# Routing to the experts in every second slot: eleven steps of a top-4 choice spread over nineteen slots of a pipelined kernel

## What is computed

```python
h = _layernorm(x) * (1 + ca) + sa
x = x + ga * attention(h)          # top 2 of 8 experts; chunks of linear attention, 8 heads
h = _layernorm(x) * (1 + cb) + sb
h = h @ lin0_w + lin0_b
h = _silu(h @ swi1_w1 + swi1_b1) * (h @ swi1_w2 + swi1_b2)
# the mixture of the feed-forward half
scores = softmax(h @ gate_w.T)
topv, topi = top_k(scores, 4)
topv = topv / sum(topv)
combine = zeros((t, 8)).at[arange(t)[:, None], topi].set(topv)
g = _silu(einsum('td,edh->eth', h, exp_w1))
u = einsum('td,edh->eth', h, exp_w3)
routed = einsum('te,etd->td', combine, einsum('eth,ehd->etd', g * u, exp_w2))
shared = _silu(h @ sh_w1) * (h @ sh_w3) @ sh_w2
h = (routed + shared) @ lin1_w + lin1_b
h = _silu(h @ swi2_w1 + swi2_b1) * (h @ swi2_w2 + swi2_b2)
x = x + gb * h
```

## Time and profile before

| what | us |
|---|---|
| median of three runs | 1185.22 |
| lowest and highest | 1184.74, 1187.0 |
| the profiled execution | 1182.44 |
| its span, first to last instruction | 1180.7 |
| TensorE busy in the span | 1038.6 |
| VectorE busy | 889.3 |
| ScalarE busy | 651.6 |
| GpSimd busy | 508.5 |

### The profile page before, as it was taken

The page is one execution under the profiler, slowest core; times in us unless marked ns, Lnnn a source line. Parts: engine busy times, 40 slices in busy tenths (PEclk is TensorE's granted clock), DMA queues, the critical chain, the costliest instruction groups (busy, mean ns, idle before and its releaser), DMA issues.

```text
span 1180.7 us, 26036 instructions
## 1 busy us (share of the span) xinstructions
PE 1038.6 (88%) x8950; PEld 759.1 (64%) x8950; DVE 889.3 (75%) x2067; ACT 651.6 (55%) x1596; POOL 508.5 (43%) x464
## 2 busy tenths in 40 slices
PE   4776778889998888999899898978998899899997
PEld 3554556656666665667666666756776677677774
DVE  3775576889996577778778887788778877886764
ACT  2432444445554555766567564756776665555564
POOL 2217144431224443221222126767886554455552
PEclk9787899999998999999999999999999999999999
DMA  8982133333332332222222116330532233225230
GB/s 232 399 349 94 67 108 104 108 101 91 99 106 91 95 100 86 68 61 71 66 71 66 56 42 177 90 94 25 158 103 59 65 100 99 61 67 151 80 90 18
DMA packets 81134, 123.08 MB, mean 104 GB/s; under 512 B 8944, under 2 KB 63728, under 8 KB 76912
## 3 DMA queue, kind: packets, MB, share of 16 engines
q1 hardware_dynamic: 70768, 96.24, 26.4%
q0 software_dynamic: 10240, 25.18, 6.8%
HBM read 70.27 MB, written 51.12 MB: 103 GB/s over the span
## 4 chain that ended last, share of the span: by engine, by line
PE 57%; DVE 23%; ACT 7%; issue 7%; another core or an unknown queue 5%; SPq 0%; DMA 0%; POOL 0%; DVEq 0%; ACTq 0%; POOLq 0%
PE wide L1410 7%; PE bank L1670 6%; PE wide L1660 6%; PE bank L1660 6%; PE bank L1385 6%; PE bank L1470 5%; PE bank L1454 3%; DVE epp L1746 3%; DVE att L1512 3%; DVE kvw L1753 2%; PE bank L963 2%; PE bank L1462 2%; PE bank L1399 2%; PE bank L1372 1%
## 5 line engine op out<-in xcount | busy, mean ns | idle before, releaser
L1625 POOL TENSOR_TENSOR kvw<-kvw,hq 128x512 f32<-128x512 f32 x128 | 173.0, 1352 | 153.0 <-ACT kvw L1713 152.7
L1512 DVE SCALAR_TENSOR_TENSOR att<-reach,endrel,wide 128x1024 f32<-128x1024 f32 x152 | 194.5, 1280 | 52.9 <-PE wide L1410 33.6
L885 POOL DMA_INDIRECT gst<-attended_rows,idxs x128 | 134.0, 1047 | 215.7 <-DVE att L1512 108.2
L255 POOL DMA_INDIRECT routed_rows<-hq,idxs x128 | 127.0, 992 | 220.0 <-DVE att L1512 110.6
L1746 DVE TENSOR_TENSOR epp<-kvw,epp 128x512 fp32r<-128x512 f32 x160 | 134.9, 843 | 87.0 <-ACT epp L1721 84.6
L1670 PE MATMUL bank<-epp,w2p 128*128 128x512 f32 x480 | 163.5, 449 | 11.1 <-DVE epp L1746 11.1
L1721 ACT ACTIVATE epp<-kvw 128x512 fp32r<-128x512 f32 x160 | 100.7, 629 | 84.5 <-DVE kvw L1753 80.1
L1660 PE MATMUL bank<-hp,w1p 128*128 128x512 f32 x480 | 138.1, 396 | 0.0
L1660 PE MATMUL wide<-hp,w3p 128*128 128x512 f32 x480 | 136.6, 393 | 0.0
L1385 PE MATMUL bank<-kvw,turned 128*128 x304 | 129.1, 507 | 3.8 <-ACT turned L1275 1.6
L1410 PE MATMUL wide<-turned,kx 32*128 32x128 f32 x2432 | 112.5, 298 | 21.2 <-DVE att L1512 19.5
(11 more groups left out here) (267 smaller groups left out, 1878.0 us busy)
## 6 DMA issues: line engine op xcount, KB each, us to landing
hq<-weight_rows SPq DMA_DIRECT2D x16, 2048.0 KB
rows<-routed_rows SPq DMA_DIRECT2D x76, 256.0 KB
routed_rows<-zero SPq DMA_DIRECT2D x2, 7168.0 KB, 34.1
attended_rows<-ob SPq DMA_DIRECT2D x76, 128.0 KB
routed_rows<-zero SPq DMA_DIRECT2D x1, 5120.0 KB, 17.4
out<-fin SPq DMA_DIRECT2D x16, 256.0 KB, 2.3
routed_rows<-hq,idxs POOLq DMA_INDIRECT x128
gst<-attended_rows,idxs POOLq DMA_INDIRECT x128
```

What stands on the lines that cost most here:

```text
L255: pool.indirect_dma_start(hs[s], bass.IndirectOffsetOnAxis(idxs[:, t, k:k + 1], 0), hq[:, t, :], None, bounds_check=BLOCKS[s] * P - 1, oob ...
L885: pool.indirect_dma_start(gst[:, u, k, :], None, orow[s], bass.IndirectOffsetOnAxis(idxs[:, t, k % TOPA:k % TOPA + 1], 0), bounds_check=BL ...
L1512: dve.scalar_tensor_tensor(out=att[:, n % 2, :, :], in0=reach[:, :, :].rearrange("p a c -> p (a c)").unsqueeze(1) .to_broadcast([P, 4, 2 * ...
L1625: pool.tensor_tensor(g, g, rows_of(1 - b % 2, n, n + 1), ALU.mult).then_inc(s_eu, 1)
```

## The change

Part p of a group's routing stood p slots behind the group's step 0. It now stands 1 + floor(9 (p - 1) / 5) slots behind: steps 1, 2, 4, 6, 8, 10, 11, 13, 15, 17 and 19 for parts 1 to 11. The exponential (step 2) and the turn of the weights (step 21) stay.

```diff
             for part in range(1, 12):
-                r = group(part, slot)
+                r = group(1 + (part - 1) * 9 // 5, slot)
                 if r is not None:
                     route(r, part)
```

## The result

| | median us | runs | lowest to highest |
|---|---|---|---|
| before | 1184.91 | 20 | 1180.91 to 1194.32 |
| changed | 1191.27 | 20 | 1184.50 to 1205.27 |

The account below looks back on a forecast made before the run. TensorE holds plain expert slots; routing on VectorE costs about 31 us. Savings of 3.0 + 3.0 for two expert groups, 3.5 for the last and 0 for attention give 9.5, so 1175.7 us; 8 in 10 between 1168.5 and 1186.

Parts of the forecast that it names:

- the first period: First ten slots of an expert group's routing, parts 1 to 6 after the change: VectorE 4.7 us late at its end.
- stretching: VectorE's routing instructions lengthened while GpSimd multiplies: moving part 3 removes 0 to 2.5 us per expert group, taken as 1.3.
- The room of the second period: Next ten slots of an expert group, parts 7 to 11: VectorE's idle time there saves 1.7 us a group.
- Part 7 "free in digit 3": Slots whose number ends in 3, where VectorE waits 2.09 us: part 7 there adds nothing.
- a slot with idle time hides a stretched instruction at least in part: Part 3's new slot, where VectorE waits: reason for taking 1.3 us saved, between bounds 0 and 2.5.
- Parts 10 and 11 at 0.64 each: Two two-instruction parts late in the second ten slots of an expert group: each adds 0.64 us of VectorE lateness.
- New waits: TensorE's turn of the weights: waits for part 11 in the last group, already waits for logits elsewhere; 0, at most 1.3 us.
- Part 3 behind the tail's step: Last group: VectorE's tail step now precedes part 3, so TensorE's 3.58 us wait falls to around 1, keeping its clock.
- The last group, "saved 3.5": Third expert group's routing, slots 93 to 113: cost falls from 7.5 to 4.0 us, bounded by 0.7 and 7.5.
- The exponential's 2.45 that stays: Slot with part 2, such as slot 14: ScalarE's exponential makes it 2.45 us longer than plain, before and after.
- The attention loop: Its twenty slots with routing, where 3.3 of 10.6 us show: no change, bounds -2 to +1.5 us.
- The rival: Routing parts each meet GpSimd's multiplication and gathers and stretch by 1 us: slower, 1192 us, chance 0.09.

## Why the prediction was wrong

In the first group the first period came as forecast, and the second did not. By my account the first was to be 4.6 us shorter (3.3 of parts and 1.3 of stretching) and is 4.4 shorter. The second was to be 1.6 longer and is 5.6 longer. In the second group it is 3.5 shorter and 5.1 longer.

- **The room of the second period: right in kind and size, and not what decided.** I worked out 1.7 us a group; with the multiplication out of the way it is 1.2 to 1.3.
- **Part 7 "free in digit 3", and "a slot with idle time hides a stretched instruction at least in part": the step that failed.** While VectorE is idle in those slots GpSimd is at work (in digit 3 for 1.03 us of 2.09, in digit 4 and 6 throughout), and GpSimd's work is what stretches VectorE's. Three instructions of 0.29 us took 3.6 us and used up the 2.09 us of the earlier trace rows and more. Together with part 8 this is +3.1 us in slots 23 to 28, where my account had 1.28 - 1.07 + 0.4 - 0.3, +0.3. I had bounded the stretching by 0 below, "all of it stays"; it grew. Over units 13 to 43 VectorE's stretched instructions (over 0.25 us above their usual length) sum up to 12.7 us against 9.2, those of the routing to 5.2 against 2.6.
- **Parts 10 and 11 at 0.64 each: too small by 2.7 us.** I had 1.28 for the two in slots 29 to 31, and slots 29 to 35 take 4.0 more. In these slots VectorE is the chain, and with the multiplication at its full length the lateness costs more than itself, through line 1056 and through the clock's fall behind the wait at the turn.
- **New waits, "the other groups' turn already waits for the next batch's logits": true and no comfort.** The wait grew from 0.70 to 3.10. Where the clock stays up, slots 33 and 35 are plain behind a wait of 3.09; where it falls, they take 1.5 us more.
- **Part 3 behind the tail's step: right.** In the changed kernel the wait of 3.58 us at line 1684 in unit 98 falls to 0.45, at its weight load, and slot 15 is 2.30 (I said 2.3). Slot 16 was to stay under 3.1 and is 3.65 in both expert groups of this execution, with the copy still at 1.20; in other executions with part 3 in this slot it is 2.79 and the copy 0.23, as I had said, behind a slot 15 of 2.95.
- **The last group, "saved 3.5": the wrong way.** Slots 93 to 103 are 1.5 us shorter, and slots 104 to 113 are 3.7 longer. 1.3 of that is slot 105, with part 8 and line 1083 stretched to 1.27 (I had about 1.1 for a part there), 1.5 are slots 109 and 111 with parts 10 and 11, and 0.6 is slot 113 with the turn. My 4.0 was no sum but a choice between two bounds, and the cost is 9.1 (54.8 less 45.7), above the upper one. A new wait of 2.13 at line 1684 follows behind slot 105, at 1055 us, one batch after the one that went, and TensorE's clock falls to 0.50 behind it, from 1056.1 to 1059.5: the low stretch moved, where I had it gone.
- **The exponential's 2.45 that stays: too large.** It is 1.4 a group, by the run without it; as a term in both sums it does not touch the difference.
- **The attention loop: no change within bounds;** 116.1 us for its last thirty slots against 115.0 (I had -2 to +1.5).
- **The rival** that decided is the third, at 0.09: stretching in the parts that now stand apart. I had it decide above half of the parts. Three of the seven parts were enough (3, 7 and 8, with six long instructions in the first group), since the room was worth only 1.7.

## What to carry to other kernels

An engine's idle time in a slot is free for added work only if the work doesn't need what the others are using in that slot. So look at what the other engines do in the idle time before filling it. In this kernel many short VectorE instructions beside GpSimd's long ones were dear, since each that met one waited for its end, however short it was itself. That held for those with two inputs in SBUF and for line 1089's copy. Keeping them to slots in which GpSimd rests was not tried. Where a pipeline's chain already passes through the engine, work costs the same or more wherever in that part it stands: parts 10 and 11 cost 1.4 us there with the multiplication short, and 4.0 with it.

## What was not expected of the hardware

- A VectorE instruction on 8 elements, 0.17 us alone, takes 1.22 to 1.27 us in slot 15 beside GpSimd's long instructions; one on 128 elements up to 1.27 in the changed kernel (lines 1083 and 1093). In slot 23 the length is set by GpSimd's instruction, and VectorE's ends 0.14 or 0.15 us behind it.
- A wait of TensorE of 3.1 us was followed by 3.4 us at 0.50 of the clock in one execution and by none in another. In the run with the last two parts late, one execution has both: 0.50 behind the wait of 3.10 us, full clock behind that of 2.54.
